# GpSimd's work of an LSTM step waits for the step's f32 h, not for its low part

## What is computed

```python
def step(carry, xw_t):            # 64 times, x: (32, 64, 256)
    prev_h, prev_c = carry
    a = xw_t + prev_h @ Wh        # (32, 1024): i, f, o, g of 256 each
    next_c = sigmoid(f) * prev_c + sigmoid(i) * tanh(g)
    next_h = sigmoid(o) * tanh(next_c)
...
h = s0 * dense(k0, concat([h, -h]));  h = relu(h) * 2     # 1024 wide
h = s1 * dense(k1, h);                h = relu(h) * 2     # 1024 wide
y = x + s2 * dense(k2, h)                                 # 256 wide
```

## Time and profile before

| what | us |
|---|---|
| median of 3 runs | 268.54 |
| lowest and highest | 268.23, 269.05 |
| the profiled execution, its own time | 268.54 |
| its span, from first to last instruction | 266.7 |

### The profile page before, as it was taken

The page is one execution under the profiler, slowest core; times in us unless marked ns, Lnnn a source line. Parts: engine busy times, 40 slices in busy tenths (PEclk is TensorE's granted clock), DMA queues, the critical chain, the costliest instruction groups (busy, mean ns, idle before and its releaser), DMA issues.

```text
span 266.7 us, 8593 instructions
## 1 busy us (share of the span) xinstructions
PE 263.0 (99%) x3360; PEld 195.9 (73%) x3360; DVE 226.1 (85%) x842; ACT 190.5 (71%) x596; POOL 78.7 (30%) x107
## 2 busy tenths in 40 slices
PE   8999999999999999999999999999999999999996
PEld 5888788878889888888888886876766444444444
DVE  3898888899999999998989999788877699992573
ACT  4787987888978888888889878888773677323220
POOL 0022010002434534544534522432322283040210
PEclk9999999999999999999999999999999999999999
DMA  6990000000000000000000001000001010000004
GB/s 206 322 381 6 2 2 0 2 4 2 2 4 1 4 2 2 2 5 2 2 2 2 4 4 39 2 4 2 2 26 56 2 39 1 0 2 1 0 0 157
DMA packets 5288, 8.71 MB, mean 33 GB/s; under 512 B 640, under 2 KB 2944, under 8 KB 5120
## 3 DMA queue, kind: packets, MB, share of 16 engines
q1 hardware_dynamic: 4960, 7.64, 8.3%
q10 hardware_dynamic: 288, 0.52, 0.6%
HBM read 6.07 MB, written 2.10 MB: 31 GB/s over the span
## 4 chain that ended last, share of the span: by engine, by line
PE 89%; DVE 7%; ACT 2%; DMA 1%; issue 0%
PE WK L777 16%; PE WK L840 10%; PE WK L821 9%; PE WK L760 8%; PE GFO L739 5%; PE G L739 5%; PE G L730 5%; PE GFO L730 4%; PE WK L860 4%; PE ACC L840 4%; PE WK L878 3%; PE GFO L840 3%; PE ACC L777 2%; DVE aT L1384 2%; PE GFO L878 2%; PE ACC L760 2%
## 5 line engine op out<-in xcount | busy, mean ns | idle before, releaser
L1000 ACT ACTIVATE tT<-aT 128x64 f32<-128x64 f32 x189 | 44.9, 269 | 22.1 <-DVE aT L1384 14.6
L777 PE MATMUL WK<-h,k 128*128 128x256 f16 (+1 forms) x360 | 51.9, 288 | 0.0
L1384 DVE TENSOR_REDUCE aT<-GFO 128x64 f32<-128x128 f32 x128 | 36.5, 285 | 5.6 <-PE GFO L739 3.6
L777 PEld LDWEIGHTS WK<-h,k 128*128 128x128 fp8e5 x360 | 33.6, 98 | 7.8
L760 PE MATMUL WK<-xs,wxs 128*128 128x512 f32 x138 | 36.8, 401 | 0.0
L739 PE MATMUL GFO<-h,w 128*128 128x64 f16 x504 | 35.1, 192 | 0.0
L760 PEld LDWEIGHTS WK<-xs,wxs 128*128 128x128 f32 x138 | 24.9, 188 | 4.6
L1384 DVE TENSOR_REDUCE aT<-G 128x128 f32<-128x256 f32 x64 | 27.1, 424 | 0.0
L730 PEld LDWEIGHTS G<-h,w 128*128 128x128 f16 x504 | 17.3, 96 | 12.2 <-DVE h L1502 8.7
L739 PE MATMUL G<-h,w 128*128 128x64 f16 x504 | 25.0, 193 | 0.0
L993 ACT ACTIVATE GFO<-xw 128x256 f32<-128x256 f32 x63 | 23.3, 370 | 0.0
(11 more groups left out here) (223 smaller groups left out, 574.3 us busy)
## 6 DMA issues: line engine op xcount, KB each, us to landing
x<-in_x SPq DMA_DIRECT2D x3, 512.0 KB, 8.8
xw<-in_wh SPq DMA_DIRECT2D x4, 256.0 KB, 5.2
k<-in_k SPq DMA_DIRECT2D x1, 1024.0 KB, 10.5
out_y<-x SPq DMA_DIRECT2D x8, 128.0 KB, 1.8
out_y<-x SPq DMA_DIRECT2D x3, 256.0 KB, 2.1
xw<-in_wx SPq DMA_DIRECT2D x4, 128.0 KB, 4.4
x<-in_x ACTq DMA_DIRECT2D x2, 256.0 KB, 3.8
xw<-in_wx SPq DMA_DIRECT2D x2, 256.0 KB, 5.4
```

The lines of the kernel that those rows point to most:

```text
L777: ins = eng.matmul(layer_src(tile), w, rhs, start=a == 0, stop=last)
L1000: eng.activation(tT[:, B * j0:B * j1], aT[:, j0:j1].rearrange("p j b -> p (j b)"), ACT.Tanh, scale=half_gain0 if t == 0 else half_gain).th ...
L1384: eng.tensor_reduce(aT[:, j0:j1], G[g][:, 0:64 * (j1 - j0)].rearrange("p (j h b) -> p j b h", h=2, b=B), op=ALU.add, axis=AX.X).then_inc(a ...
```

## The change

GpSimd's wait at the head of a step asks for `h32_made`, which L1503 raises, in place of `hl_made`, which L1505 raises. Both count one per step, and the value asked for is the same. Nothing else differs: every engine has the same instructions in the same order.

```diff
             for t in range(T):
                 if pool_plan[t] or t in (X2_HI_STEP, X3_HI_STEP):
-                    eng.wait_ge(hl_made, t + 1)
+                    eng.wait_ge(h32_made, t + 1)
                 if t == X2_HI_STEP:
                     for k in range(2):
                         x_hi(2, k)
```

## The result

| | us |
|---|---|
| before, median of 17 runs | 268.59 |
| after, median of 17 runs | 269.31 (268.87 to 269.94) |
| ratio after to before | 1.0028, 95% interval 1.0017 to 1.0039 |
| profiled execution after: its time, its span | 269.02, 267.2 |

The changed kernel is slower by 0.28%, some 0.7 us, with an interval of 0.17% to 0.39%. The forecast was 269.7 us and "slower".

What follows compares the result with a forecast made beforehand. The chain of 64 LSTM steps was taken to bound the kernel. Costs of 1.00 + 0.33 + 0 less a gain of 0.16 give 1.17 us, so 268.54 + 1.17 = 269.7 us; range 268.1 to 270.6.

Steps and rivals of the forecast that it cites:

- the race: Head of a step: L1505, starting 0.05 us before GpSimd, was to reach SBUF first and keep its 0.22.
- The gain: Steps 27, 44 and 45: L1484 no longer waits for GpSimd's second operation, 0.06 + 0.05 + 0.05 = 0.16 us.
- The cost: After steps 17, 19, 21, 23 and 0, L1260 or L1216 waits for one GpSimd operation: 1.00 + 0.33 us.
- The 0.09 that TensorE absorbs after step 21: In the step after step 21 TensorE is 0.09 us late anyway, so this much of the delay is absorbed.
- Step 4: L1418 held, h 0.18 us late, hidden by TensorE's late start after step 5: cost 0, or up to 0.2.
- rule 2: If GpSimd is first, VectorE's operation ends its own time less 0.13 us after GpSimd's end.
- Results that come earlier are worth nothing by themselves: All steps: no matmul was seen waiting for GpSimd, so only where GpSimd's work lies beside VectorE's counts.
- TensorE's start after L1502: TensorE's start on the new h, 0.29 us after L1502 in a quiet step; later where other matmuls remain.
- the first rival: After the costly steps VectorE's next operation goes ahead of GpSimd, only the 0.16 stands: 268.4 us; chance 0.22.
- That VectorE's next operation keeps its turn: L1260, issued 0.08 us before L1505's end, stays ahead of GpSimd: 268.4 us; chance 0.22.
- rule 1: If VectorE is first, GpSimd's operation ends as if it had started 0.14 us before VectorE's end.
- That the pair goes through: GpSimd's second operation also runs ahead of the waiting VectorE one, 0.6 us more per costly step: 273 us; chance 0.03.

Runs made afterwards that it cites:

- the mixed kernel: The changed kernel, but GpSimd waits for L1505 again in steps 0, 4, 17, 19, 21 and 23; 268.32 us, ratio 0.9979 to before.
- the next two experiments: Kernel before with GpSimd's early start in steps 17, 19, 21 and 23 alone (ratio 1.0033), and in steps 0 and 4 alone (1.0013).
- the race kernels: Changed kernel with an idle VectorE addition of 64, 96, 112 or 128 columns between L1503 and L1505; 269.85, 270.63, 272.97 and 302.23 us.
- 64, 96 and 112 columns: Changed kernel with an idle VectorE addition of that width between L1503 and L1505; 269.85, 270.63 and 272.97 us.

## Why the prediction was right

**The bound and the race.** GpSimd starts 0.045 after L1505 (0.05 was said), L1505 takes 0.22 to 0.23 in all steps, and GpSimd's operation is 0.04 longer. The race was won by more than was thought, for the reason above.

**The gain** of L1484 was put at 0.16 and is 0.17.

**The cost.** L1260 was to take 0.87 to 0.90 and takes 0.86 to 0.90; L1216 was to take 1.11 and takes 1.10. The stretches cost 0.23, 0.26, 0.26, 0.27 and, for step 0, 0.30, where 0.25, 0.28, 0.28, 0.28 and 0.33 were said. Each is 0.01 to 0.03 smaller, mostly because h follows the delayed reduction after 1.79 us (from 21.80 to 23.59 in step 0) and not after 1.81. The 0.09 that TensorE absorbs after step 21 came as said. Step 4 is free, as said, but not in the way that was said. Its h was to come 0.18 late and TensorE's late start to hide that. It came 0.03 late: L1418 ends 0.28 after the cast, and not 0.41. The casts before step 0 already had a VectorE operation of this kind, L1203, 0.28 behind GpSimd's end, and L1203 takes 0.48 where nothing holds it (in the mixed kernel). So rule 2, taken from operations that read two tensors, doesn't fit those that read one tensor and scalars. The lateness was put too large, and the slack behind it was hardly needed: here the right figure is in part luck.

**What was missed.** "Results that come earlier are worth nothing by themselves" was wrong. It rested on the waits view, which doesn't show TensorE waiting for GpSimd. In two steps TensorE did wait, for 0.17 and 0.05 us, and the changed kernel gets 0.11 back there. The prediction's own measure, TensorE's start after L1502, had the sign of it in the kernel before: 0.44 and 0.33 after h of steps 33 and 59, where 0.28 is the least. The last 0.12 are spread over 50 stretches by a few ns each. The kernel with an early start in steps 32 and 58 alone has 0.14 of the same kind in steps that it leaves alone, and the mixed kernel and those of the next two experiments have 0.07 to 0.09. So it isn't an effect of the change: the one profiled execution of the kernel before is that much longer than the others. What makes it so stays open. A small misreading changed nothing: the chain, from the first L1502 to the last, is 182.8 of 266.7 us, 69% of the span and not three quarters.

**The sum.** By the stretches it is 1.33 - 0.09 - 0.17 - 0.11 - 0.12, or +0.83 with rounding, in the profiled executions; 1.17 was said. By the medians it is 0.72, with an interval of 0.17% to 0.39%, or 0.5 to 1.0 us. The 0.44% of the forecast lie just above it: the mechanism was right, and the size was 1.4 times that of the stretches and 1.6 times that of the medians. Of the 0.34 too much, 0.23 are the two terms that the prediction put at nothing (0.11 of it real, 0.12 drift), and 0.10 the costs. The measured 0.28% also lies below the 0.3% that was called the least a measurement can tell, to which 0.1 was given; with 17 runs of each kernel it could be told. And the stated range held the first rival's 268.4 and an unchanged time too, so the time alone would not have singled out this mechanism. L1260's 0.86 does.

**The rivals.** That VectorE's next operation keeps its turn didn't happen. The lead was called thin, 0.06, and the race kernels show that a VectorE operation may start up to about 0.03 behind and still win, so it was thinner still: 0.06 against a turn between 0.028 and 0.037. L1260 may have lost by that, or because GpSimd had been waiting since 0.045 after L1505's start, long before the start that rule 1 counts. No run separates these two for L1260, and I leave it there. That the pair goes through didn't happen either: L1260 and L1216 waited for one operation each, and the second one waited for them. The rule of the Trainium skill ("SBUF — State Buffer", "Who interferes with whom") that the first has the shared ports for its whole instruction would have given 268.4. The trace says otherwise on the length of the hold: GpSimd gets in before L1505's recorded end, ahead of an L1260 that started 0.08 before that end.

## What to carry to other kernels

A wait that isn't there for data may still be there for order. Before it is moved forward, list what the other engine runs in the next microsecond and ask of each operation whether it reads two tiles of SBUF: such an operation and a GpSimd operation that reads SBUF take turns, and the loser waits for nearly the whole of the winner's. Operations that read one tensor with per-partition scalars can be held too, as L1418 (0.54 to 0.83) and L1203 were. Here six steps held the whole loss and the others a small gain, so choosing step by step gave a kernel faster than before (ratio 0.9979), where the change everywhere gave a slower one (1.0028). And that the waits view names no wait of TensorE doesn't prove that none exists: compare the spacing of its matmuls.

## What the runs showed of the hardware

- VectorE and GpSimd, both reading SBUF: VectorE is served first even if it starts 28 ns after GpSimd, and GpSimd if VectorE starts 37 ns or more after it. The turn between the two is sharp: all 54 steps of a kernel fall on one side but for those whose lead differs.
- An operation of VectorE that waits is served between two GpSimd operations in a row, and one of GpSimd that waits between two of VectorE in a row. Neither goes hungry; each waits for one operation of the other.
- A memset of GpSimd, which only writes, holds nothing up: L1260 at 0.42 with it, 0.86 with a subtraction.
- Of a VectorE operation with two tensors that loses, all but 0.13 to 0.15 of its own time comes after GpSimd's end (0.86 = 0.58 until that end + 0.42 - 0.13, within 0.01), so a short operation of 0.22 ends 0.08 after it. L1418, which reads one tensor and two scalars, ends 0.28 after it with 0.54 of its own.
- A GpSimd operation that loses ends as if it had started 0.14 before the recorded end of VectorE's. With 64, 96 and 112 columns L1505 ends later by 0.03 at the first step and by 0.02 at the second, and GpSimd's operation of 0.67 takes 0.73, 0.76 and 0.77.
